# Feed-forward values written to PSUM, and an instruction between a row sum and its reciprocal

## The reference

```python
for i in range(DEPTH):                      # 6
    x = attn_layer(shift_tokens(x), Wqkv[i], q_scale[i], k_scale[i], Wo[i]) + x
    x = ffn_layer(shift_tokens(x), ln_g[i], ln_b[i], W1[i], b1[i], W2[i], b2[i]) + x

def ffn_layer(x, g, bln, W1, b1, W2, b2):
    mu = x.mean(-1, keepdims=True)
    var = ((x - mu) ** 2).mean(-1, keepdims=True)
    xn = (x - mu) / jnp.sqrt(var + 1e-05) * g + bln
    hg = xn @ W1 + b1
    a, gate = jnp.split(hg, 2, -1)
    return a * jax.nn.gelu(gate, approximate=False) @ W2 + b2
```

## Time and profile before

| | |
|---|---|
| median of 3 runs | 2878.83 us (2873.51 to 2882.35) |
| profiled execution, span from first to last instruction | 2876.3 us |
| PE busy | 2709.0 us, 94% |
| DVE busy | 2616.4 us, 91% |
| ACT busy | 2273.1 us, 79% |
| POOL busy | 2115.9 us, 74% |
| granted TensorE clock, mean | 0.988 |

### The profile page before, as it was taken

One profiled execution on the slowest core, in us unless ns is written; L12 is line 12 of the kernel. 1 busy time (PEld: TensorE's weight loads), 2 busy tenths in 40 slices (PEclk: granted clock), 3 DMA queues, 4 the chain that ended last, 5 costly groups with the idle time before them and its releaser, 6 DMA issues.

```text
span 2876.3 us, 92923 instructions
## 1 busy us (share of the span) xinstructions
PE 2709.0 (94%) x36417; PEld 2060.1 (72%) x36417; DVE 2616.4 (91%) x3375; ACT 2273.1 (79%) x3824; POOL 2115.9 (74%) x1529
## 2 busy tenths in 40 slices
PE   8799978999999999999999999999999999999996
PEld 7577756777777777777777777777777777777774
DVE  6899968999999999999999999999999999999993
ACT  5799857878787887878788887878888787877873
POOL 5766658777778777777777787777777777877771
PEclk9899999999999999999999999999999999999998
DMA  1000013222223232232232233222322322322222
GB/s 57 23 2 2 1 36 76 70 71 65 71 63 76 71 76 64 66 78 67 67 76 68 66 74 73 69 67 68 75 68 66 78 65 63 72 67 58 63 66 78
DMA packets 103719, 178.41 MB, mean 62 GB/s; under 512 B 29350, under 2 KB 52708, under 8 KB 103396
## 3 DMA queue, kind: packets, MB, share of 16 engines
q1 hardware_dynamic: 102372, 174.60, 25.0%
q10 hardware_dynamic: 1152, 1.20, 0.1%
HBM read 22.62 MB, written 2.10 MB: 9 GB/s over the span
## 4 chain that ended last, share of the span: by engine, by line
POOL 26%; issue 24%; DVE 15%; PE 11%; ACT 5%; DMA 2%; POOLq 0%; DVEq 0%; SPq 0%; ACTq 0%
POOL spare L1454 15%; DVE spare L1285 5%; POOL pr L1492 4%; DVE qk_t L1294 3%; POOL spare L1463 3%; PE pa L843 3%; DVE ss L1278 3%; PE px L872 3%; DMA kT<-spare 2%; POOL xs_lo L1440 2%; DVE oT_lo L1354 1%; PE pg L982 1%; PE pg L930 1%; PE px L917 1%; POOL w_lo L1485 1%
## 5 line engine op out<-in xcount | busy, mean ns | idle before, releaser
L1454 POOL TENSOR_TENSOR spare<-spare,qk_t 128x1024 f32<-128x1024 f32 x384 | 910.2, 2393 | 11.5 <-POOL xs_lo L1440 8.1
L843 PE MATMUL pa<-w_hi,xs_hi 128*128 128x512 f32 x1152 | 511.8, 444 | 27.5 <-issue 8.4
L1470 POOL TENSOR_TENSOR sm<-sm,inv 128x512 f32<-128x512 f32 x192 | 201.8, 1051 | 446.7 <-DVE sm L1316 372.7
L1294 DVE TENSOR_TENSOR qk_t<-pa,rot 128x1024 f32<-128x1024 f32 x384 | 464.4, 1210 | 1.9 <-ACT spare L1048 1.7
L1285 DVE TENSOR_TENSOR spare<-pa,rot 128x1024 f32<-128x1024 f32 x384 | 464.5, 1210 | 0.0
L1278 DVE TENSOR_REDUCE ss<-spare 128x16 f32<-128x1024 f32 x384 | 457.5, 1191 | 6.7 <-ACT spare L1041 5.9
L843 PE MATMUL pa<-w_hi,xs_lo 128*128 128x512 f32 x1152 | 456.7, 396 | 0.0
L843 PE MATMUL pa<-w_lo,xs_hi 128*128 128x512 f32 x1152 | 454.9, 395 | 0.0
L872 PE MATMUL px<-ident_sb,spare 128*128 128x128 f32 x3072 | 409.0, 276 | 22.3 <-POOL spare L1463 11.6
L1463 POOL TENSOR_TENSOR spare<-spare,inv 128x1024 f32<-128x1024 f32 x192 | 365.9, 1906 | 80.6 <-ACT inv L1080 75.7
L872 PEld LDWEIGHTS px<-ident_sb,spare 128*128 128x128 f32 x3072 | 341.6, 141 | 111.0 <-issue 59.0
(11 more groups left out here) (180 smaller groups left out, 5970.0 us busy)
## 6 DMA issues: line engine op xcount, KB each, us to landing
kT<-spare SPq DMA_DIRECT2D x384, 256.0 KB, 3.7
pT<-prT SPq DMA_DIRECT2D x768, 64.0 KB, 2.0
w_part<-in_Wqkv SPq DMA_DIRECT2D x40, 192.0 KB, 3.7
wo<-in_Wo SPq DMA_DIRECT2D x6, 512.0 KB, 5.4
c_h<-in_x SPq DMA_DIRECT2D x4, 512.0 KB, 9.0
spare<-in_x SPq DMA_DIRECT2D x8, 256.0 KB, 5.0
out<-spare SPq DMA_DIRECT2D x8, 256.0 KB, 2.5
wo<-in_W SPq DMA_DIRECT2D x6, 341.0 KB, 5.2
```

The costliest lines, as they stand in the source:

```text
L843: last = pe.matmul(pa[(u + c) % 2][:, half * 512:half * 512 + 512], x[:, j * P:(j + 1) * P], w[:, at], start=(k == 0), stop=(k == 2))
L1294: dve.tensor_tensor(halves(qk_t[:, c, :]), halves(pa[(3 * j + c) % 2][:])[:, :, ::-1, :], table.unsqueeze(1).to_broadcast([P, HEADS, 2, DH ...
L1454: pool.tensor_tensor(qk_r[:, c, :], qk_r[:, c, :], qk_t[:, c, :], ALU.add)\
L1470: pool.tensor_tensor(keys(sm[:]), keys(sm[:]), over(inv[:, j % 2, 0, :], S), ALU.mult)\
```

## The change

`scale_shift` writes its result to the PSUM bank `pg` instead of the SBUF buffer `fx`, and the rounding and the subtraction read it from there. And the sum of `denominators` is parted from its reciprocal: the sum goes ahead of `add_attention`, `normalise` or `gated(0)`, the reciprocal stays behind them.

```diff
-                        act.activation(fx[:], fx[:], ACT.Identity, scale=ln_par[:, 0:1], bias=ln_par[:, 1:2])\
+                        act.activation(pg[:], fx[:], ACT.Identity, scale=ln_par[:, 0:1], bias=ln_par[:, 1:2])\
                             .then_inc(s["fn_ready"], 1)
...
-                        act.copy(fn_hi[:], fx[:]).then_inc(s["fn_hi_ready"], 1)
+                        act.copy(fn_hi[:], pg[:]).then_inc(s["fn_hi_ready"], 1)
...
                         dve.reduce_sum(den[:], keys(pr[:]), AX.X).then_inc(s["den_done"], 1)
+
+                def reciprocals(i, j, back):
+                    n, j, live = tile(i, j, back)
+                    if live:
                         dve.wait_ge(s["den_done"], n + 1)
                         wait_for(dve, s["probs_done"], n)
                         dve.reciprocal(rden[:], den[:]).then_inc(s["rden_done"], 1)
...
-                        dve.tensor_tensor(fn_lo[:], fx[:], fn_hi[:].bitcast(F32), ALU.subtract).then_inc(s["fn_lo_ready"], 1)
+                        dve.tensor_tensor(fn_lo[:], pg[:], fn_hi[:].bitcast(F32), ALU.subtract).then_inc(s["fn_lo_ready"], 1)
...
                         sum_squares(i, j, 0, 1, "sq_k", "sum_k")
+                        denominators(i, j, 2)
                         if j == 3:
                             add_attention(i, 1)
                         if j == 0:
                             normalise(i, 2)
                         if j == 1:
                             gated(i, 2, 0)
-                        denominators(i, j, 2)
+                        reciprocals(i, j, 2)
                         rest_of_outputs(i, j, 3)
```

## The result

The changed kernel takes 2901.6 us in the median of four runs (2897.16 to 2903.64), against 2876.69 for the kernel before on the same chip: the ratio is 1.0079, with a 95% interval of 1.0064 to 1.0094. It is slower by some 23 us; I had forecast 2884, within 0.3% of no change, and the range ended at 2895.

The account below looks back on a forecast made before the run. Bound: a loop of waits between nearly full engines. Terms -0.45 - 0.05 + 0.35 + 0.19 = +0.04 us a group (+0.29 in 12 of 46 rounds), +5 us in all: 2884 us; 8-in-10 range 2862 to 2895.

Parts of the forecast that it names:

- (e): Second step: sum ahead of the gating makes PE's block and scores late; +0.19 us a group, bounds -0.11 to +0.48.
- (d): First step, sum ahead of `normalise`: adds nothing, since ACT is already late; about 0.1 us without the fourth step's lateness.
- (a): First step, `fn_lo` split on DVE: one operand in PSUM saves 0.45 us a group, bounds -0.52 to 0.
- (b): First step, ACT's scaling and rounding through PSUM: together -0.05 us a group ahead of `fn_lo`, bounds 0 to -0.10.
- (c): Fourth step: sum ahead of the attention's addition makes ACT's list late to `fn_hi`; +0.35 us a group, bounds 0 to 0.60.
- The 0.11 us a step of the reciprocal: Between sum and reciprocal on DVE, each of three steps: 0.11 us saved by parting, up to 15.8 us if each counted.
- PE's loss in the second step: Rival, second step: PE can't catch up behind its block, costing +0.48 us a group; 2894 us, chance 0.19.
- The late addition was not hidden: Rival, fourth step: ACT catches up before `fn_hi`, lateness costs 0; 2870 us, 2856 with gating hidden too; chance 0.29.
- the PSUM operand did help: Rival denied here, first step: `fn_lo` stays at 1.13 us, half of the 0.45 stays; +10 us, 2893, chance 0.07.

## Why the prediction was wrong

**The step that failed is (e), the parting in the second step.** I wrote +0.19 us, and for the bounds -0.11 to +0.48. It measured +0.62 us in the step (12.00 to 12.62 over PSUM alone) and 0.13 more in the fourth, 28 us in the kernel. What I priced there, the late gating through PE's block and scores, is 7 us when measured by itself, 0.20 us a group by the groups. That this meets my 0.19 is partly luck: only 0.09 of it stands in the second step, and 0.12 in the fourth, at PE's scores, where I had let PE's idle time take the lateness up. What I did not price is the wait that comes with putting the sum first: the sum needs the exponential. In (d) I asked whether the sum's input is done at its new place, for the first step; for the second, where it isn't, I never asked. The instruction that I moved back had been the cover. The missed wait is 21 us by itself and 16 in the whole change (1.0079 - 1.0024), where the forecast missed by 18.

**(a) PSUM for the split: right in mechanism and price, a third of it not kept.** 1134 to 692 ns, against 1.13 to 0.68 predicted. I counted the 0.45 us in the loop as if all of DVE's path behind `fn_lo` moved with it. The gating of the second step, though, also waits for PE's blocks behind the gelu, and they hang on the rounding, not on `fn_lo`. The kernels without the gelu show that: 0.48 us a group there, 0.31 with it (18 and 10 us by the medians). The rule of the Trainium skill on PSUM sources, which I had weighed against the step, is not borne out by this case: 692 ns with PSUM, 691 at the least without.

**(b) ACT's two instructions: right.** 0.80 and 0.58 us, -0.07 together against -0.05 (medians 827 to 798 and 619 to 581 ns).

**(c) The late addition: right in mechanism, too large in size.** +0.35 us predicted; measured alone +0.22 us in the first step, 0.23 in the group and 11 us in the kernel, and on top of the second step's parting 0.09 with the first step's. DVE's wait for the output split went to 2.33 us (2.2 forecast), and the wait before `fn_lo` to 0.46 (0.6 forecast).

**(d) The first step's parting: right.** Nothing, measured apart.

**The 0.11 us a step of the reciprocal** never counted, as forecast for the first and fourth steps.

Put right from the groups of the runs, the sum reads: -0.31 for PSUM as far as it was kept, +0.23 for the late addition, +0.20 for the late gating and +0.55 for the missed wait: +0.67 us a group, against +0.53 measured. The 0.14 between them is overlap: with the second step parted, the other two partings add 0.09 and not 0.23. Of the rivals, the one that came nearest, in number and in sign, is PE's loss in the second step (2894): DVE does wait for the scores ahead of the third step's transpose now, 0.23 us, but mostly because all of the gating came later still. With the late gating alone that wait is 0.15 us in the median, in half the groups. The late addition was not hidden, and the PSUM operand did help.

## What to carry to other kernels

When an instruction is moved ahead of another, look up when each of its inputs arrives at its new place, in every step of the loop where it is moved; an input that was in time by the length of the instruction now behind it makes a wait that stalls the whole list. A gain on one engine is kept only as far as the next meeting with another engine's list, so follow every input of the next instruction behind it, and ask which of them did not move. And a pair of instructions with a wait of 0.1 us between them is cheap against 0.6 us of lateness for whoever waits on the one in the middle.

## What the runs showed of the hardware that was not expected

A DVE subtraction with both operands in SBUF costs what POOL leaves it: of 128x512 elements it took 691 to 1211 ns. In the kernel before, 46 of the 48 start while POOL multiplies (`norm_probs`, also from and to SBUF), and all 46 end 0.546 to 0.555 us after POOL's instruction ends; the two that find POOL idle take 691 and 692 ns. With the parting alone the split starts later, POOL's instruction has less left, and it takes 1008 ns in the median; 46 of 48 again end 0.544 to 0.553 us after POOL's. The wait lies inside the recorded duration, so no view of waits shows it. The longest split of the kernel before, and the shortest beside POOL of the kernel with the parting alone:

```profile
...
803.68 1.06 POOL L1492 TENSOR_TENSOR pr<-pr,rden 128x512 f32<-128x512 f32 x1
...
804.08 1.21 DVE L1348 TENSOR_TENSOR fn_lo<-fx,fn_hi 128x512 fp32r<-128x512 f32 x1 [0.23 <-ACT fn_hi L1194]
...
```

```profile
...
1719.89 1.05 POOL L1497 TENSOR_TENSOR pr<-pr,rden 128x512 f32<-128x512 f32 x1
...
1720.80 0.70 DVE L1352 TENSOR_TENSOR fn_lo<-fx,fn_hi 128x512 fp32r<-128x512 f32 x1 [0.88 <-ACT fn_hi L1194]
...
```

With one operand in PSUM it takes 691 to 693 ns in all 48 cases of the changed kernel, 46 of them beside the same work of POOL. The Trainium skill, "SBUF — State Buffer", section "Who interferes with whom", says that a DVE instruction with two SBUF inputs contends with a GpSimd instruction that reads SBUF, and one with at most one SBUF input does not; the traces agree, with 1134 ns in the median against 692. No run here varied POOL's own work.
